# First batch's keys in groups of four through root, scaling and transposes; slot evictions on ScalarE alone; GpSimd's slot fill in pieces

## Chip, cores and metric

The kernel runs on one core of one Trainium2 chip. The metric is the device time of the program in microseconds, the median of the runs; lower is better. Engines are named as the profile names them: PE (TensorE), DVE (VectorE), ACT (ScalarE), POOL (GpSimd), SP (SyncE, which issues the DMAs here).

## What is computed

Two layers of gated cross attention and feed-forward on `x` (4 batches, 256 tokens, 256 wide), with a context of 1601 tokens of width 128 per batch. The change lies wholly in the first layer's attention:

```
y_main, y_dca = y[:, :-16], y[:, -16:]                 # 1585 and 16 context tokens
kv_dca = (y_dca @ Wkv_dca + bkv_dca).reshape(b, 16, 2, H, HD)   # H = 16 heads of HD = 16
k_dca, v_dca = _ln(kv_dca[:, :, 0], kn_dca_w, kn_dca_b), kv_dca[:, :, 1]
q = _ln((x @ Wq + bq).reshape(b, s1, H, HD), qn_w, qn_b)
...        # k, v of y_main likewise, with kn_w, kn_b
_attn(q, k, v) = softmax(q k^T * HD**-0.5) v           # over both sets of keys, apart, then added
```

`_ln` normalises each head's 16 numbers of each token. The mean is taken out in the weights beforehand, so per key and head there remain a sum of squares, a root, a reciprocal and a product. The rest (a mixture of 16 experts, a second attention with 16 heads of 128, a feed-forward with ternary weights) is the same before and after.

## The kernel before

A planner (`Plan`) writes one list of pieces in program order. Every engine walks the list and emits its own part of each piece with semaphore waits, so each engine runs a fixed order. `Plan.stage0` makes the order of the first layer's attention. Its generator `prep(b, banks)` prepares a batch; the loop around it takes one or two steps of `prep` for each step of the scores, and as many steps of `maxima` as the pace wants. For batch 0 the loop runs 19 steps of lead in which there are no scores yet: the kernel's first 100 us. Five of the eight PSUM banks (0, 1, 2, 3, 7) carry the pieces of this preparation, 4 and 5 the maxima.

The pieces of batch 0's preparation, in the order before:

- `kv` (14 of them): a key and value tile of 128 context tokens (tile 12 has 65, tile 13 is the 65-row tail again with the other weights). PE makes `[128, 512]` in a bank; DVE adds the bias to the key half on its way to `kc` (L1315, which reads `wk` from SBUF), then ACT copies the value half to `va` (L1633) and frees the bank.
- `sq`, `ss`: ACT squares four tiles (L1646), DVE sums sixteens into `ss` (L1332). There are five groups: tiles 0 to 3, 4 to 7, 8 to 11, 12 and 13, and the two query tiles.
- `ln1`, `ln2`, `ln3`, `q`: statistics of the tokens (DVE L868, L870), their root (ACT L890), the normalising (DVE L876, L883), the turn on PE (L906) and its copy (ACT L894), and the queries' matmuls with their eviction (DVE L1325).
- `sqrt`: one square root over all of `ss` (ACT L1652), when all five sums are there.
- `scale` (5): DVE takes the reciprocal of a group (L1339) and multiplies the tiles by it (L1342). The queries come first.
- `qt`, `kt`: PE transposes four tiles' half (L999, L1008), ACT writes the result twice, in fp32 and in bf16 (L1660, L1663; L1673, L1674). `qsplit`, `ksplit`: the difference of the two, by DVE (L1364) or GpSimd (L1875) in turn.
- `qr`, `kr`: PE multiplies the split keys by a selection matrix `rsb` and so puts them into the slots of `kst`: eight indices p, each with three tiles of 512 columns and one of 65 (49 main, 16 dca keys). Evictions: `kr` tiles 0, 1, 2 on ACT (L1698), but tile 3 of every p and tile 1 of every odd p on DVE (L1371, L1372; L1375). `qr` by ACT (L1691).
- `bvt`, `bvo`: a bias row through `wo`; then the scores begin.

Later batches get their slots by DMA (`kd`) from SP; their bank `kst1` needs marks in it, which GpSimd writes at the start. Ahead of the list each engine has a few single instructions. On DVE these are the centring of the weights (L1278, L1280), a memset of bank 6 (L1283), and this:

```
for i in range(2):
    V.tensor_scalar(vd[0:TAIL, i, :, 16:17], va[i][0:TAIL, 0, :, 16:17], prm[0:TAIL, 8:9], None,
                    ALU.mult).then_inc(vd_ones, 1)
```

On GpSimd they are memsets and the fill of `kst1` (L1834), one instruction of 8 x 1585 elements per partition and one of 8 x 16, then an add for the bias row (L1837). On ACT they are the tanh of the gates (L1617) and the cast of `rsb` (L1619), both waiting for loads.

## Time and profile before

| | |
|---|---|
| median of three runs | 1677.91 us |
| all three | 1680.65, 1677.91, 1677.08 us |
| the profiled execution's own time | 1681.94 us |
| its span | 1680.6 us |
| its mean granted TensorE clock | 0.945 |
| busy: PE, DVE, ACT, GpSimd | 1460.4, 1244.0, 1101.0, 794.4 us |

The span runs from the first to the last instruction. Busy time of an engine contains time in which a started instruction stands still, so a high share is no proof of work. The granted clock is 1.00 at 2.4 GHz and 0.50 at 1.2 GHz; values between are means over a stretch. A line number is that of the kernel before; several engines share L599, the helper of all matmuls.

### The profile page before, as it was taken

To read this page: it belongs to the slowest core of one execution; us is meant where nothing else is said; L and a number is where in the kernel's file an instruction comes from. 1 tells how busy PE (TensorE), PEld (TensorE's weight loads), DVE (VectorE), ACT (ScalarE), POOL (GpSimd) and SP (SyncE) were. 2 spreads that over 40 slices of the span, in tenths; PEclk is the share of its full clock that TensorE was granted. 3 is DMA by queue.
4 is the path that set the end of the run, shared out by engine and by line. 5 is a ranking of instruction groups with operands and counts; after the bars stand their busy time and mean duration, and the time that the engine had idled before them with its cause. 6 is when DMAs were issued, how large, how long until landed. Compare 5 with 4: busy or idle time off the path is not lost.

```text
span 1680.6 us, 25444 instructions
## 1 busy us (share of the span) xinstructions
PE 1460.4 (87%) x8460; PEld 711.5 (42%) x8460; DVE 1244.0 (74%) x2229; ACT 1101.0 (66%) x1996; POOL 794.4 (47%) x618
## 2 busy tenths in 40 slices
PE   5688887888878797788898989899899999999979
PEld 3243343343333343344444444344544455455445
DVE  6767667667786256478887768899589997788937
ACT  3556656756754755477786668678477775788724
POOL 3014013013130001077766749787486876577823
PEclk8798998998989999799999999999999999999989
DMA  4001200300340100100001000000000000000000
GB/s 154 1 1 29 52 2 2 60 1 2 60 176 1 51 1 5 40 20 6 1 1 32 29 21 6 26 1 1 5 26 1 26 1 1 1 1 1 1 0 26
DMA packets 20489, 36.70 MB, mean 22 GB/s; under 512 B 4898, under 2 KB 15238, under 8 KB 19334
## 3 DMA queue, kind: packets, MB, share of 16 engines
q1 hardware_dynamic: 20358, 35.07, 7.2%
q8 instruction: 68, 1.11, 0.3%
q14 instruction: 63, 0.52, 0.1%
HBM read 26.53 MB, written 1.15 MB: 16 GB/s over the span
## 4 chain that ended last, share of the span: by engine, by line
PE 35%; POOL 9%; issue 7%; DVE 5%; ACT 3%; POOLq 0%; DMA 0%; ACTq 0%; DVEq 0%; SPq 0%
PE BK L599 35%; POOL arena L1929 6%; DVE arena L1559 2%; DVE arena L1542 1%; ACT arena L1806 1%; ACT arena L1814 1%; POOL arena L1926 1%; POOL arena L1904 1%; ACT arena L1799 1%; POOL arena L1935 1%; POOL arena L1914 1%; DVE arena L926 0%; PE BK L906 0%; ACT L1799 0%; DVE arena L1573 0%
## 5 line engine op out<-in xcount | busy, mean ns | idle before, releaser
L599 PE MATMUL BK<-arena 128*128 128x512 bf16 (+14 forms) x8130 | 1414.1, 375 | 188.8 <-DVE arena L1380 43.4
L599 PEld LDWEIGHTS BK<-arena 128*128 128x128 bf16 (+7 forms) x8130 | 674.2, 115 | 897.7 <-issue 218.5
L1929 POOL TENSOR_TENSOR arena<-arena 128x512 f32<-128x512 f32 (+1 forms) x352 | 509.1, 1446 | 178.7 <-ACT arena L1799 154.6
L1559 DVE TENSOR_TENSOR arena<-arena 128x512 bf16<-128x512 f32 (+1 forms) x416 | 513.9, 1244 | 39.8 <-ACT arena L1806 39.1
L1799 ACT ACTIVATE arena<-BK,arena 128x512 f32<-128x512 f32 (+1 forms) x416 | 285.9, 687 | 131.7 <-PE BK L599 116.1
L1707 ACT ACTIVATE arena<-BK 128x512 f32<-128x512 f32 (+1 forms) x416 | 227.2, 604 | 95.0 <-PE BK L599 89.6
L1380 DVE TENSOR_REDUCE arena<-BK 128x1 f32<-128x512 f32 x384 | 244.2, 682 | 53.1 <-PE BK L599 52.2
L1806 ACT CAST arena<-arena 128x512 bf16<-128x512 f32 (+1 forms) x416 | 253.3, 609 | 0.0
L1814 ACT ACTIVATE arena<-BK 128x512 bf16<-128x512 f32 (+1 forms) x256 | 130.0, 508 | 87.7 <-PE BK L599 87.6
L1542 DVE CUSTOM_DVE_ANT_0 arena<-BK,arena 128x512 bf16<-128x512 f32 (+1 forms) x256 | 145.5, 568 | 47.4 <-PE BK L599 41.8
L1848 POOL TENSOR_TENSOR arena<-arena 128x256 f32<-128x256 f32 (+6 forms) x45 | 30.2, 671 | 184.1 <-ACT arena L1646 181.7
L1875 POOL TENSOR_TENSOR arena<-arena 128x512 bf16<-128x512 f32 x24 | 28.2, 1176 | 114.6 <-ACT arena L1674 101.7
L1926 POOL TENSOR_TENSOR arena<-arena 128x512 f32<-128x512 f32 x32 | 45.3, 1417 | 63.5 <-ACT arena L1799 63.5
L1894 POOL TENSOR_TENSOR arena<-arena 128x512 f32<-128x512 f32 x2 | 2.5, 1268 | 117.0 <-DVE arena L1500 117.0
L1507 DVE TENSOR_TENSOR arena<-BK,arena 128x512 f32<-128x512 f32 x32 | 22.0, 687 | 45.9 <-ACT arena L1759 45.7
L1633 ACT COPY arena<-BK 128x256 f32<-128x256 f32 (+1 forms) x52 | 18.9, 372 | 56.1 <-DVE arena L1315 56.1
L1935 POOL TENSOR_TENSOR arena<-arena 128x512 f32<-128x512 f32 x32 | 43.7, 1365 | 9.4 <-DVE arena L1564 9.2
L1315 DVE TENSOR_TENSOR arena<-BK,arena 128x256 f32<-128x256 f32 (+1 forms) x56 | 23.0, 420 | 32.3 <-PE BK L599 32.2
L1579 DVE SCALAR_TENSOR_TENSOR arena<-BK,arena 128x256 f32<-128x256 f32 x8 | 3.9, 484 | 53.6 <-PE BK L599 53.6
L1859 POOL TENSOR_TENSOR arena<-arena 128x1024 f32<-128x1024 f32 (+2 forms) x15 | 23.4, 1591 | 29.6 <-DVE arena L848 29.6
L1788 ACT CAST arena<-BK 128x512 bf16<-128x512 f32 x32 | 18.7, 585 | 25.0 <-PE BK L599 25.0
L1914 POOL TENSOR_TENSOR arena<-arena 128x384 bf16<-128x384 f32 (+1 forms) x20 | 19.7, 1005 | 31.2 <-ACT arena L1781 31.2
(175 smaller groups left out, 850.1 us busy)
## 6 DMA issues: line engine op xcount, KB each, us to landing
arena<-arena SPq DMA_DIRECT2D x144, 50.0 KB, 2.2
arena<-in_ctxT SPq DMA_DIRECT2D x8, 800.5 KB, 4.4
arena<-in_ctxk SPq DMA_DIRECT2D x4, 768.0 KB
arena<-in_wo SPq DMA_DIRECT2D x1, 2048.0 KB, 7.5
arena<-in_wqT SPq DMA_DIRECT2D x1, 2048.0 KB, 7.8
arena<-in_x SPq DMA_DIRECT2D x4, 256.0 KB, 9.4
arena<-in_rsel SPq DMA_DIRECT2D x1, 1024.0 KB, 9.1
arena<-in_rw1T SPq DMA_DIRECT2D x1, 1024.0 KB, 5.0
```

Source lines behind the costliest of these rows:

```text
L599: return T.matmul(out_, lhsT, rhs, start=start, stop=stop, skip_group_check=True)
L1380: V.tensor_reduce(mxp[:, g % 2, u, c:c + 1], BK[i][:, :], AX.X, ALU.max).then_inc(free[i], 1)
L1542: V.tensor_tensor_reduce(out=junk[:, 0:w], in0=BK[i][:, 0:w], in1=rl[:, k % 3, 0:w], scale=1.0, scalar=-3e38, op0=ALU.add, op1=ALU.max, ac ...
L1559: V.tensor_tensor(Pl[k][0:m, :], P1[k][0:m, :], Ph[k][0:m, :], ALU.subtract).then_inc(p_low, 1)
L1707: A.activation(P0[(2 * s + r) % NP][0:m, :], BK[i][0:m, :], ACT.Exp, scale=0.25).then_inc(free[i], 1)
L1799: A.activation(P1[k][0:m, :], BK[i][0:m, :], ACT.Exp, scale=SCALE1, bias=mcb[0:m, b, kt:kt + 1]).then_inc(free[i], 1)
L1806: A.copy(Ph[k][0:m, :], P1[k][0:m, :]).then_inc(p_high, 1)
L1814: A.activation(rl[:, k % 3, 0:w], BK[i][:, 0:w], ACT.Relu).then_inc(free[i], 1)
L1914: t = G.tensor_tensor(ckl[0:m, b, w_, :], ckf[0:m, w_, :], ckh[0:m, b, w_, :], ALU.subtract)
L1926: G.tensor_tensor(acc[:, g % 2, :], P1[(s - 1) % NR][:, :], P1[k][:, :], ALU.add).then_inc(summed1, 1)
L1929: G.tensor_tensor(acc[0:m, g % 2, :], acc[0:m, g % 2, :], P1[k][0:m, :], ALU.add).then_inc(summed1, 1)
L1935: G.tensor_tensor(dg[:, :, :], idn[:, :].unsqueeze(1).to_broadcast([128, 4, 128]), dn[:, 4:8].unsqueeze(2).to_broadcast([128, 4, 128]), AL ...
```

## The change

1. `first_batch` replaces the batch-0 half of `prep`. Each group of four tiles goes on by itself: square, sum, root (`sqrt` now has a group index), reciprocal and scaling, transposes of the first half, splits, while later key tiles are still being made. The queries' group comes last. The statistics of batches 1 to 3 are put between those steps, their roots (`lr`) between the slot evictions of the second half. The second half's transposes follow the first half's slots, as before.
2. The split counters are renumbered for batch 0 (`q_split`, `k_split`): the query split comes after the first half's.
3. All slot tiles of `kr` are evicted by ACT.
4. DVE's two tensor_scalars on `vd` are gone; GpSimd writes the same values with one copy, ahead of the fill. The fill of `kst1` becomes one instruction of 8 x 16 and eight of 1585, after the bias add.
5. On ACT the tanh moves behind `bvt`, the cast of `rsb` to just before the first square.

```diff
+        def first_batch(bank, qs):
...
+            def slots(hf):
+                for p in range(4 * hf, 4 * hf + 4):
+                    if p % 2 == 0:
+                        piece("qr", 0, p, bank=bank())
+                        yield
+                    for c in range(4):
+                        piece("kr", 0, p, c, bank=bank())
+                        if c == 3:
+                            known.add((0, p))
+                        yield
+                    if hf and p < 7:
+                        piece("lr", 0, p - 3)
+
+            for kt in range(6):
+                keys(kt)
+                if kt == 3:
+                    piece("sq", 0, 0)
+                yield
+            piece("ss", 0, 0)
+            next(qs)
...
+            piece("sq", 0, 1)
+            piece("sqrt", 0, 0)
+            keys(8)
+            next(qs)
+            yield
+            keys(9)
+            piece("ss", 0, 1)
+            yield
+            piece("scale", 0, 1)
+            next(qs)
+            keys(10)
+            yield
+            keys(11)
+            piece("sqrt", 0, 1)
+            piece("sq", 0, 2)
+            next(qs)
+            yield
+            turned(0, 0)
+            keys(12)
+            piece("scale", 0, 2)
...
+            piece("ksplit", 0, 0, 3)
+            piece("scale", 0, 0)
+            piece("ln1", 0, 2)
+            yield
+            piece("qt", 0, bank=bank())
+            yield
+            piece("qsplit", 0)
+            piece("ln1", 0, 3)
+            yield
+            yield from slots(0)
+            for c in range(4):
+                turned(1, c)
+                yield
+                piece("ksplit", 0, 1, c)
+            yield
+            yield from slots(1)
...
-            dve.wait_ge(va_ones, 6)
-            dve.wait_ge(ld_prm, 16)
-            for i in range(2):
-                V.tensor_scalar(vd[0:TAIL, i, :, 16:17], va[i][0:TAIL, 0, :, 16:17], prm[0:TAIL, 8:9], None,
-                                ALU.mult).then_inc(vd_ones, 1)
...
-                elif kind == "kr":
-                    b, p, c = arg
-                    if c == 3 or (c == 1 and p % 2):
-                        dve.wait_ge(full[i], n + 1)
...
-            act.wait_ge(ld_g, 16)
-            A.activation(tg[:, :], gat[:, :], ACT.Tanh).then_inc(tanh_done, 1)
-            act.wait_ge(ld_rs, 16)
-            A.copy(rsb[:, :, :, :].rearrange("p a b n -> p (a b) n"), rsf).then_inc(rsb_done, 1)
...
-                    A.activation(ss[:, :, :], ss[:, :, :], ACT.Sqrt, scale=1.0 / 16, bias=cst[:, 1:2]).then_inc(ss_root, 1)
+                    act.wait_ge(*summed(j))
+                    A.activation(ss[0:m, lo:hi, :], ss[0:m, lo:hi, :], ACT.Sqrt, scale=1.0 / 16,
+                                 bias=cst[0:m, 1:2]).then_inc(ss_root, 1)
...
+                    o = kst[b % 2][:, p, :]
+                    act.wait_ge(full[i], n + 1)
+                    if c == 3:
+                        A.activation(o[:, 1536:NMAIN], BK[i][:, 0:TMAIN], ACT.Identity, bias=prm[:, 10:11])
+                        A.activation(o[:, NMAIN:S2], BK[i][:, TMAIN:TAIL], ACT.Identity, bias=prm[:, 11:12]).then_inc(free[i], 1)
+                    else:
+                        A.activation(o[:, 512 * c:512 * c + 512], BK[i][:, :], ACT.Identity, bias=prm[:, 10:11]).then_inc(free[i], 1)
...
-            for lo, hi, col in ((0, NMAIN, 10), (NMAIN, S2, 11)):
-                G.tensor_copy(kst1[:, :, lo:hi], prm[:, col:col + 1].unsqueeze(2).to_broadcast([128, 8, hi - lo])
-                              ).then_inc(k_marked, 1)
+            G.tensor_copy(vd[0:TAIL, :, :, 16:17].rearrange("p i h o -> p (i h) o"),
+                          prm[0:TAIL, 8:9].unsqueeze(2).to_broadcast([TAIL, 32, 1])).then_inc(vd_ones, 2)
...
+            for p in range(8):
+                G.tensor_copy(kst1[:, p:p + 1, 0:NMAIN], prm[:, 10:11].unsqueeze(2).to_broadcast([128, 1, NMAIN])
+                              ).then_inc(k_marked, 1)
```

How the instructions move, at three places. First DVE, from the memset of bank 6 on. Before:

```order
L1283 MEMSET BK 128x512
L1287 TENSOR_SCALAR arena<-arena 65x16 x2
L1315 TENSOR_TENSOR arena<-BK,arena 128x256 x4
L1332 TENSOR_REDUCE arena<-arena 128x64
L1315 TENSOR_TENSOR arena<-BK,arena 128x256 x2
```

In the changed kernel (its key eviction is L1397, its sum L1414):

```order
L1370 MEMSET BK 128x512
L1397 TENSOR_TENSOR arena<-BK,arena 128x256 x6
L1414 TENSOR_REDUCE arena<-arena 128x64
L955 BN_STATS arena<-arena 128x6
L957 BN_AGGR arena<-arena 128x2
```

The two tensor_scalars are gone, six key evictions instead of four come ahead of the first sum, and the token statistics follow it. Second, DVE again, where groups are scaled. Before, from the last statistics on (L1339 is the reciprocal, L1342 the product):

```order
L868 BN_STATS arena<-arena 128x6
L870 BN_AGGR arena<-arena 128x2
L1339 RECIPROCAL arena<-arena 128x32
L1342 TENSOR_TENSOR arena<-arena 128x512
L1339 RECIPROCAL arena<-arena 128x64
L1342 TENSOR_TENSOR arena<-arena 128x1024
L1339 RECIPROCAL arena<-arena 128x64
```

In the changed kernel (L1421 reciprocal, L1424 product, L1407 a query tile's eviction, L1401 that of the dca values):

```order
L1414 TENSOR_REDUCE arena<-arena 128x64
L1421 RECIPROCAL arena<-arena 128x64
L1424 TENSOR_TENSOR arena<-arena 128x1024
L1397 TENSOR_TENSOR arena<-BK,arena 128x256 x2
L1407 TENSOR_TENSOR arena<-BK,arena 128x256
L1397 TENSOR_TENSOR arena<-BK,arena 65x256
L1421 RECIPROCAL arena<-arena 128x64
L1424 TENSOR_TENSOR arena<-arena 128x1024
L1407 TENSOR_TENSOR arena<-BK,arena 128x256
L1397 TENSOR_TENSOR arena<-BK,arena 65x256
L1401 TENSOR_SCALAR arena<-BK,arena 65x16x16
L1414 TENSOR_REDUCE arena<-arena 128x64
```

The product of the first full group now stands after tile 9 and ahead of the eviction of tiles 10 and 11, that of the second between tiles 12 and 13. Third, ACT at the start of the slots. Before (L1691 is a query slot, L1698 a key slot tile; the remaining key tiles are DVE's):

```order
L1682 ACTIVATE arena<-BK,arena 128x16
L1684 ACTIVATE arena<-BK,arena 128x16
L1691 CAST arena<-BK 128x512
L1698 ACTIVATE arena<-BK,arena 128x512 x5
L1691 CAST arena<-BK 128x512
L1698 ACTIVATE arena<-BK,arena 128x512 x5
L1673 ACTIVATE arena<-BK,arena 128x512
L1674 ACTIVATE arena<-BK,arena 128x512
```

In the changed kernel (L1763 query slot, L1772, L1769, L1770 key slots, L1732 and L1735 the transposed queries):

```order
L1754 ACTIVATE arena<-BK,arena 128x16
L1756 ACTIVATE arena<-BK,arena 128x16
L1732 ACTIVATE arena<-BK,arena 128x512
L1735 ACTIVATE arena<-BK,arena 128x512
L1763 CAST arena<-BK 128x512
L1772 ACTIVATE arena<-BK,arena 128x512 x3
L1769 ACTIVATE arena<-BK,arena 128x49
L1770 ACTIVATE arena<-BK,arena 128x16
L1772 ACTIVATE arena<-BK,arena 128x512 x3
L1769 ACTIVATE arena<-BK,arena 128x49
L1770 ACTIVATE arena<-BK,arena 128x16
```

The transposed queries come right ahead of the slots, and each index p has three wide evictions and two narrow ones on ACT. On PE the order from the first `qr` to the first score is the same in both kernels.

## Rows read from the trace of the kernel before

**Rows 1.** Windows: us, busy time (instructions) of each engine, granted clock, DMA share, GB/s.
```profile
20.30:59.70 39.40, 20.18 (x70) 14.38 (x71) 25.54 (x56) 19.10 (x38) 3.58 (x4) 0.67 0.07 21
...
59.70:95.00 35.30, 30.01 (x132) 10.80 (x132) 26.80 (x61) 20.53 (x34) 1.15 (x1) 0.85 0.01 1
...
100.50:560.00 459.50, 387.83 (x3434) 166.18 (x3433) 316.61 (x676) 289.87 (x555) 100.18 (x116) 0.92 0.14 35
```

**Rows 2.** DVE's timeline, 9 to 22 us: start, us, what, count.
```profile
9.99 10.39 DVE L1287 TENSOR_SCALAR arena<-arena 65x16 f32<-65x16 f32 x2
...
20.29 1.40 DVE L1315 TENSOR_TENSOR arena<-BK,arena 128x256 f32<-128x256 f32 x4
```

**Rows 3.** GpSimd's timeline, before the loop and at 110 us.
```profile
8.92 11.43 POOL L1834 CAST arena<-arena 128x12680 bf16<-128x12680 f32 x2 [6.29 <-DMA arena<-in_prm]
...
51.78 1.66 POOL L1875 TENSOR_TENSOR arena<-arena 128x512 bf16<-128x512 f32 x1 [30.67 <-ACT arena L1674]
...
109.52 2.54 POOL L1848 TENSOR_TENSOR arena<-arena 128x512 f32<-128x512 f32 x3 [32.35 <-ACT arena L1646]
```

**Rows 4.** PE's timeline (in brackets: idle before, and what ended it).
```profile
7.12 7.32 PE L599 MATMUL BK<-arena 128*128 128x256 f32 x20 [7.12 <-DMA arena<-in_ctxT]
...
21.22 7.74 PE L599 MATMUL BK<-arena 128*128 128x256 f32 x24 [6.78 <-ACT arena L1633]
...
32.46 0.87 PE L906 MATMUL BK<-arena 128*128 128x128 f32 x4 [3.51 <-ACT arena L1633]
...
54.70 1.01 PE L599 MATMUL BK<-arena 128*128 128x256 bf16 x4
...
59.72 6.34 PE L599 MATMUL BK<-arena 128*128 128x512 bf16 x25 [4.01 <-DVE arena L1364]
```

**Rows 5.** Windows of 1 us, PE alone: us, busy, granted clock, DMA share, GB/s.
```profile
19.00:20.00 1.00, 0.00 (x0) 0.53 0.00 0
...
25.00:26.00 1.00, 1.00 (x4) 0.56 0.00 0
...
33.00:34.00 1.00, 1.00 (x5) 0.50 0.00 0
```

**Rows 6.** DVE by shape, 0 to 100.5 us: count, busy us, mean ns, idle before.
```profile
L1342 DVE TENSOR_TENSOR arena<-arena 128x1024 f32<-128x1024 f32 x3 | 3.7, 1224 | 0.1
...
L1332 DVE TENSOR_REDUCE arena<-arena 128x64 f32<-128x1024 f32 x3 | 3.7, 1220 | 5.2 <-ACT arena L1646 5.2
...
L1339 DVE RECIPROCAL arena<-arena 128x64 f32<-128x64 f32 x3 | 1.6, 544 | 0.0
...
L1342 DVE TENSOR_TENSOR arena<-arena 65x512 f32<-65x512 f32 x1 | 1.3, 1267 | 0.0
...
L1342 DVE TENSOR_TENSOR arena<-arena 128x512 f32<-128x512 f32 x1 | 0.7, 692 | 0.0
```

**Rows 7.** ACT by shape, 0 to 100.5 us.
```profile
L1698 ACT ACTIVATE arena<-BK,arena 128x512 bf16<-128x512 f32 x20 | 13.6, 688 | 12.0 <-PE BK L599 11.9
...
L1673 ACT ACTIVATE arena<-BK,arena 128x512 f32<-128x512 f32 x6 | 4.7, 778 | 5.0 <-DVE arena L1364 3.0 <-PE BK L1008 2.0
...
L1646 ACT ACTIVATE arena<-arena 128x1024 f32<-128x1024 f32 x3 | 3.2, 1062 | 0.0
...
L890 ACT ACT_TABLE_LOAD x1 | 1.3, 1283 | 0.7 <-DVE arena L870 0.7
...
L1679 ACT ACTIVATE arena<-BK,arena 128x49 bf16<-128x49 f32 x2 | 0.8, 400 | 0.0
```

**Rows 8.** DVE by shape, 0 to 100.5 us: its slot evictions.
```profile
L1375 DVE TENSOR_SCALAR arena<-BK,arena 128x512 bf16<-128x512 f32 x4 | 3.0, 749 | 0.9 <-PE BK L599 0.9
...
L1371 DVE TENSOR_SCALAR arena<-BK,arena 128x49 bf16<-128x49 f32 x8 | 2.1, 260 | 3.0 <-PE BK L599 3.0
...
L1372 DVE TENSOR_SCALAR arena<-BK,arena 128x16 bf16<-128x16 f32 x8 | 1.8, 224 | 0.0
```

**Rows 9.** DVE's timeline at 111 us.
```profile
111.65 0.42 DVE L1315 TENSOR_TENSOR arena<-BK,arena 128x256 f32<-128x256 f32 x1 [0.44 <-PE BK L599]
```

More of the change, by code:

```diff
@@ L99, in prep @@
             qs = queries()
+            if b == 0:
+                yield from first_batch(bank, qs)
+                return
             for kt in range(NKT + 1):
@@ L115, in prep @@
             piece("ss", b, 4)
-            if b:
+            yield
+            yield
+            for part in range(4):
+                piece("nw", b, part)
                 yield
-                yield
-                for part in range(4):
-                    piece("nw", b, part)
-                    yield
-            else:
-                for later in range(1, B):
-                    piece("ln1", 0, later)
-                yield
-                piece("sqrt", b)
             for r in range(5):
@@ L1666, in scalar_main @@
                     b, hf_, c = arg
[L1667 removed]
+                    u = k_split(b, hf_, c)
                     act.wait_ge(full[i], n + 1)
```

135 lines of the change are left out of this document (78 added, 57 removed).

## Prediction, made before the changed kernel was run

> **What bounds the kernel now.** I read the windows of the first 100 us first, then each engine's timeline there, then the instructions by shape, and last the waits. The kernel is one in-order program per engine, and the only stretch the change reorders is the first batch's key preparation, before the long loop. First look at DVE [rows 2]: two tensor_scalars of 65x16 elements that write a column of ones into `vd` and take 10.39 us together. Ops of 16 elements elsewhere take about 0.2 us [rows 8]. They start at 9.99 and end at 20.38; the first GpSimd fill of `kst1` runs from 8.92 to 20.35 [rows 3]. So DVE stands still until GpSimd lets go of something, and the key tiles' evictions are queued behind it. PE computes the five key tiles that its banks hold, stops at 14.44 and resumes at 21.22 [rows 4]. In that idle time its granted clock falls from 2.4 to 1.2 GHz, and it is back at about 25.9 us [rows 5].
>
> From 20.3 to 59.7 us nothing is saturated: DVE 25.5 of 39.4 us, ACT 19.1, PE 20.2 [rows 1]. It is a relay: all squares, all sums, one square root, then reciprocal and scaling of each group, transposes, splits. PE gets the first slot matmul at 59.72 [rows 4]. From there to the bias transpose at 95.0 PE is busy 30.0 of 35.3 us, DVE 26.8, ACT 20.5 [rows 1]: PE and DVE (the maxima) alternate as the limit. After 100 us neither the instructions nor their order change, and no load waits for an absolute time, so I take an earlier start as an earlier end, one to one.
>
> **The stall (gain).** The two ops leave DVE; the ones are written by GpSimd, as one small copy ahead of the fill. DVE is free after its memset, about 10.1 us, instead of 20.4. Its next work is the key evictions, 1.40 us for four [rows 2]. They read one operand from PSUM and one from SBUF. Does a GpSimd instruction hold them too? [rows 9] say no: the eviction at 111.65 takes 0.42 us while GpSimd's adds run from 109.52 to 112.06. An op with both inputs in SBUF is another matter: the scaling of 65x512 took 1267 ns against 692 for the larger 128x512 one [rows 6], and it ran at 52.7 beside a GpSimd subtract of 1.66 us [rows 3]. The Trainium skill (SBUF — State Buffer, "Who interferes with whom") has the same division: a Vector instruction contends if it is in a two-port mode, or has two SBUF inputs while GpSimd reads SBUF, and the loser blocks fully. By that rule the new order has one exposed place, the two normalising tensor_scalars about 21 us, if the fill is still running; by it the sum would be one piece of the fill, 1.4 us, less gain.
>
> The fill in nine pieces costs the same, 11.2 us over eight large pieces, 1.4 us each, ending about 21.5. Nobody needs it before the second batch's slot DMAs; what the pieces bound is any hold, to 1.4 us instead of 11.4. I put no hold into the sum and keep 1.4 us for the range.
>
> **The walk to the first slot matmul.** Per-piece times: a key tile on PE. Five took 7.32 us. The next six took 7.74 us, 4.7 of them at 1.2 GHz and 3.1 at 2.4 [rows 4, 5]; with a the price at full clock, 4.7/2a + 3.1/a = 6, so 0.9 us at full clock and 1.8 at half. Square of four tiles 1.06, pair of copies of a transposed slab 1.5, table load 1.28 [rows 7]; sum 1.22, reciprocal 0.54, scaling 1.22 [rows 6]; square root of a group 0.3 to 0.4, as ACT's 49-wide ops [rows 7].
> 1. Key tiles 0 to 3 are evicted as PE gives them; ACT then has the 1.9 us cast of `rsb` (moved behind the copies; it was idle time before) and the first square: to 17.1. PE goes on at full clock through tile 9, about 19.
> 2. Norm statistics, table load, root: 21.1. Apply, PE turn: 23. First group: sum to 18.3, second square 22.8, root 23.1, reciprocal and scaling on DVE to 25.7. PE has idled again from 19 to 22, and in the trace a gap of 3.5 us before 32.5 was followed by a fall to half clock [rows 4, 5], so I price tiles 10 to 13 and the queries low: last tile full at 32.6 (at full clock 29.5).
> 3. Groups three, four and the queries now each run round ACT (square), DVE (sum), ACT (root), DVE (reciprocal, scaling), PE (transpose), ACT (two copies), DVE (split), in a fixed order: third group scaled 32.2, fourth 37.0, tail 41.4, queries 44.5.
> 4. Query transposes 1.1, ACT 1.5, the split on GpSimd 1.2 to 1.7 [rows 3], slot queries 1.0 [rows 4], less a little that overlaps: first slot matmul at 49.5. With tiles at full clock and no wait at the hand-offs, 45.
>
> A check from the other side: DVE's own work in that order, from the memset to the queries' scaling, adds up to about 22 us. At the density that DVE had in the old relay (25.5 in 39.4, 65%) that is 34 us, ending at 44, and 4.7 us of step 4 give 48.8. If DVE never waited, it would be 37. I take 47.5, between the two values of the walk; before it is 59.72. **Gain 12.2 us**, with 10 and 15 as ends, and 22 as the far bound.
>
> Two edits cost nothing: tanh moves behind the bias transpose, where the table for exp was loaded already, and ACT is not the late engine there; the number of ACT's table loads is unchanged. The roots of batches 1 to 3 leave the path (their statistics too: half of them now stand behind the queries' scaling) and are put between slot evictions, three small ACT ops.
>
> **The slot phase.** All 32 slot tiles of the batch are evicted by ACT now; PE's order does not change. DVE loses 3.0 + 2.1 + 1.8 = 6.9 us [rows 8], down to 19.9. ACT takes four more 512-wide at 0.69, eight 49-wide and eight 16-wide at about 0.4 [rows 7], and the three roots: 2.8 + 6.4 + 0.9, so 20.5 becomes 30.6 in a stretch that lasted 35.3 us. PE has 30.0. So the limit passes from PE and DVE to PE and ACT. Were both to overlap perfectly, 4.5 us would be gained; if ACT waits as DVE did, there is a loss of some 2 us. One index costs ACT 3 x 0.69 + 2 x 0.4 = 2.9 us, so the first half, where it has little beside, becomes ACT's (11.6 us for four indices) and should neither win nor lose; the second, which is full of maxima on DVE, should win. I take **2 us gained**.
>
> **Sum.** 12.2 + 2 = 14.2. The profiled execution took 1681.94 us (span 1680.6), so its counterpart is 1667.7; it stands 4 us above the median of the three runs, 1677.91, from which the same sum gives **1663.7**. About 0.2%, 3.4 us, is what a measurement of this kernel tells from no change.
>
> **Rivals.**
> - *Only the stall goes* (0.17). The group-wise relay pays for its hand-offs, four crossings between ACT and DVE per group, and ACT evicting alone eats the rest: start at 50, slot phase 1.5 us longer. For it: in the old relay, too, the engines were idle a third of the time. Gain 8: 1670.
> - *DVE-bound start* (0.10). PE keeps its 2.4 GHz through the keys because it no longer idles 6.8 us; first slot matmul at 44, slot phase 4 us shorter: gain 20, 1658.
> - *Evictions are held after all* (0.04, the slower side). If the key evictions too had to wait for the fill (they read `wk` from SBUF), each would pass between two pieces, 1.4 us apart; eight get through by 21.5. The start then wins some 3 us only, and the slot phase decides: once ACT's 30.6 us plus its waits (ACT's waits for PE there are 12.0 us now [rows 7]) pass 38.3 us, the whole is slower. At their full sum of 42, it is 4 us slower: 1682. Against it stand [rows 9].
> - *The gain is taken back later* (0.05): the long loop from 100 us has PE at 388 of 460 us and a granted clock of 0.92 [rows 1]; if the shifted start changes how often PE falls to 1.2 GHz there, 12 us are 3% of that stretch. The three runs lie within 3.6 us, which speaks against it. Result within 0.2% of 1677.9.
>
> **Numbers.** Forecast case 0.64, gain 11 to 17. Range: the forecast and the first two rivals, with the far bounds left out: 1658 to 1670.5. Faster by over 0.2%: 0.64 + 0.17 + 0.10 = 0.91; within 0.2%: 0.05; slower: 0.04.
>
> **What would show it.** DVE's first key eviction starts at 10 to 10.5 us and takes 0.4; no DVE op before 100 us lasts over 1.6 us; GpSimd shows eight casts of 1.4 us. PE's first idle stretch is near 19 us, not 14.4. First slot matmul 45 to 50 (56 or later: the relay did not shorten). Bias transpose at 78 to 83. From there on the distance between the two traces stays constant to within 2 us; if it does not, the one-to-one carry is wrong. ACT busy in the slot phase about 30 us, DVE about 20; PE's waits there name ACT's slot evictions if ACT is the limit.

## The result, and the profile of the changed kernel

| | before | changed |
|---|---|---|
| median | 1679.28 us (4 runs, 1677.08 to 1680.98) | 1664.46 us (4 runs, 1664.19 to 1665.00) |
| span of the profiled execution | 1680.6 us | 1663.3 us |
| its mean granted clock | 0.945 | 0.945 |

The ratio is 0.9919 with an interval of 0.9899 to 0.9938. The medians are 14.8 us apart; the ratio, which is estimated over all runs and isn't the quotient of the medians, is worth 13.6 us, its interval 10 to 17. The forecast was 14.2.

The same events in both traces, in us:

| event | before | changed | moved by |
|---|---|---|---|
| first key eviction on DVE | 20.29 | 10.16 | 10.1 |
| first slot eviction on ACT | 60.77 | 50.84 | 9.9 |
| bias transpose on PE | 94.96 | 83.78 | 11.2 |
| first exp on ACT (scores start) | 100.46 | 89.28 | 11.2 |
| end of the span | 1680.6 | 1663.3 | 17.3 |

So the head gave 11.2 us, three less than forecast, and the rest of this pair of traces 6.1 us, where nothing was forecast. DVE's timeline, which answers [rows 2] (columns as there):

```profile
9.76 0.48 DVE L1370 MEMSET BK<- 128x512 f32 x1
10.16 0.41 DVE L1397 TENSOR_TENSOR arena<-BK,arena 128x256 f32<-128x256 f32 x1
...
21.47 1.34 DVE L970 TENSOR_SCALAR arena<-arena 128x256 f32<-128x256 f32 x2
...
24.77 1.23 DVE L1424 TENSOR_TENSOR arena<-arena 128x1024 f32<-128x1024 f32 x1
```

The key eviction starts as the memset ends and takes 0.41 us, though GpSimd, which answers [rows 3], is busy beside it:

```profile
8.91 0.84 POOL L1908 COPY arena<-arena 65x32 f32<-65x32 f32 x1 [6.28 <-DMA arena<-in_prm]
9.77 0.72 POOL L1911 TENSOR_TENSOR arena<-arena 128x256 f32<-128x256 f32 x1
...
10.67 11.67 POOL L1915 CAST arena<-arena 128x1585 bf16<-128x1585 f32 x8
```

PE, for [rows 4]:

```profile
7.33 11.36 PE L680 MATMUL BK<-arena 128*128 128x256 f32 x40 [7.33 <-DMA arena<-in_ctxT]
23.65 1.09 PE L993 MATMUL BK<-arena 128*128 128x128 f32 x4 [4.97 <-ACT arena L1700]
24.53 4.93 PE L680 MATMUL BK<-arena 128*128 128x256 f32 x12
...
29.74 2.75 PE L680 MATMUL BK<-arena 128*65 128x256 f32 x12
...
45.03 1.09 PE L1086 MATMUL BK<-arena 128*128 128x128 f32 x4 [2.57 <-DVE arena L1424]
48.94 9.19 PE L680 MATMUL BK<-arena 128*128 128x256 bf16 x40 [2.82 <-issue]
```

Ten tiles now run without a stop, to 18.69; before, five did. The last row begins with the query slots (128x256) and goes over into the key slots, whose first matmul starts at 49.74 (59.72 before). The 2.82 us ahead of it end 0.1 us after GpSimd's query split, which takes 1.15 us from 47.68. ACT's timeline:

```profile
10.64 1.28 ACT L1700 ACT_TABLE_LOAD   x1 [10.64 <-DVE arena L1397]
...
19.65 1.28 ACT L977 ACT_TABLE_LOAD   x1 [1.87 <-DVE arena L957]
...
50.84 0.69 ACT L1772 ACTIVATE arena<-BK,arena 128x512 bf16<-128x512 f32 x1 [0.27 <-PE BK L680]
```

The first row is new at this place. In the kernel before, the first table load stood at the tanh, at 0.73, long before the tanh itself:

```profile
0.73 1.28 ACT L1617 ACT_TABLE_LOAD   x1 [0.73 <-PEq L2295]
10.94 0.20 ACT L1617 ACTIVATE arena<-arena 128x4 f32<-128x4 f32 x1 [8.92 <-DMA arena<-in_gates]
```

Windows (columns as in [rows 1]). Of the changed kernel, the relay from about 20 us (where the old one began) to the first key slot's matmul, DVE's stretch from its memset to the queries' scaling, the slot phase from its first ACT eviction to the bias transpose, and the sixteen score groups from the first `mneg` of DVE to the last; then the last two of the kernel before:

```profile
20.00:49.74 29.74, 12.89 (x50) 9.56 (x51) 20.21 (x43) 15.11 (x31) 5.04 (x4) 0.65 0.09 28
9.76:44.89 35.13, 19.93 (x79) 15.49 (x77) 23.81 (x49) 20.09 (x38) 14.12 (x11) 0.77 0.30 109
50.84:83.78 32.94, 28.07 (x130) 10.13 (x128) 22.35 (x41) 25.93 (x56) 1.16 (x1) 0.87 0.00 0
78.74:531.61 452.87, 388.11 (x3351) 168.06 (x3352) 323.98 (x691) 286.95 (x550) 100.41 (x116) 0.91 0.14 36
```

```profile
60.77:94.96 34.19, 28.92 (x129) 10.34 (x127) 26.76 (x61) 20.40 (x33) 1.15 (x1) 0.86 0.01 1
89.58:548.80 459.22, 386.98 (x3351) 166.35 (x3352) 326.25 (x695) 284.34 (x543) 100.18 (x116) 0.92 0.14 35
```

DVE is busy for 68% of the first window, and for 68% of the second; in the old relay it was 65% [rows 1]. The relay itself didn't get shorter: from the first key eviction to the first key slot's matmul it takes 39.6 us (10.16 to 49.74), and it took 39.4 (20.29 to 59.72). It starts 10.1 us sooner and keeps its length; what it would be without the new order is seen below. The slot phase is 1.25 us shorter. What ACT and PE do in it, by shape (count, busy us, mean ns, idle before); ACT from 0 to 89.3 us, PE from 50.8 to 83.8:

```profile
L1772 ACT ACTIVATE arena<-BK,arena 128x512 bf16<-128x512 f32 x24 | 16.0, 697 | 4.9 <-PE BK L680 4.6
...
L1769 ACT ACTIVATE arena<-BK,arena 128x49 bf16<-128x49 f32 x8 | 2.4, 305 | 2.3 <-PE BK L680 2.3
...
L1770 ACT ACTIVATE arena<-BK,arena 128x16 bf16<-128x16 f32 x8 | 2.3, 282 | 0.0
```

```profile
L680 PE MATMUL BK<-arena 128*128 128x512 bf16 x47 | 15.7, 461 | 1.5 <-DVE arena L1446 1.5
L680 PE MATMUL BK<-arena 64*128 64x512 bf16 x32 | 10.5, 421 | 3.4 <-DVE arena L1451 3.1
```

PE's waits there name DVE's maxima (L1451) and its splits (L1446), never ACT's slot evictions. PE was and stays the nearly full engine, with DVE's maxima behind it.

Two questions follow. Which part of the change moves the first exp by how much? And where do the three to six us after 89 us come from: does an earlier start gain more than itself?

### The profile page after: what moved, and what is told of

It is laid out like the page before. It is cut to its first block, busy times and chain, and to the rows that moved or that the text cites. A ratio compares the mean times of both kernels' runs of the same rounds, so it can differ in the third digit from the quotient of the medians.

```text
span 1663.3 us, 25453 instructions
## 1 busy us (share of the span) xinstructions
PE 1459.2 (88%) x8460; PEld 712.2 (43%) x8460; DVE 1226.7 (74%) x2207; ACT 1108.0 (67%) x2020; POOL 795.7 (48%) x626
## 3 DMA queue, kind: packets, MB, share of 16 engines
HBM read 26.53 MB, written 1.15 MB: 17 GB/s over the span
## 4 chain that ended last, share of the span: by engine, by line
PE 35%; POOL 9%; issue 7%; DVE 5%; ACT 3%; POOLq 0%; DMA 0%; ACTq 0%; DVEq 0%; SPq 0%
PE BK L680 35%; POOL arena L2008 6%; DVE arena L1630 3%; DVE arena L1613 1%; ACT arena L1881 1%; ACT arena L1889 1%; POOL arena L2005 1%; POOL arena L1983 1%; ACT arena L1874 1%; POOL arena L2014 1%; POOL arena L1993 1%; DVE arena L1013 0%; PE BK L993 0%; DVE arena L1644 0%; ACT L1874 0%
## 5 line engine op out<-in xcount | busy, mean ns | idle before, releaser
L1451 DVE TENSOR_REDUCE arena<-BK 128x1 f32<-128x512 f32 x384 | 244.3, 684 | 57.0 <-PE BK L680 56.0
L2005 POOL TENSOR_TENSOR arena<-arena 128x512 f32<-128x512 f32 x32 | 44.9, 1403 | 62.3 <-ACT arena L1874 62.3
L1397 DVE TENSOR_TENSOR arena<-BK,arena 128x256 f32<-128x256 f32 (+1 forms) x56 | 23.5, 422 | 36.9 <-PE BK L680 36.9
L1993 POOL TENSOR_TENSOR arena<-arena 128x384 bf16<-128x384 f32 (+1 forms) x20 | 19.7, 1006 | 32.6 <-ACT arena L1856 32.6
```

The source lines that it names most:

```text
L1451: V.tensor_reduce(mxp[:, g % 2, u, c:c + 1], BK[i][:, :], AX.X, ALU.max).then_inc(free[i], 1)
L1993: t = G.tensor_tensor(ckl[0:m, b, w_, :], ckf[0:m, w_, :], ckh[0:m, b, w_, :], ALU.subtract)
L2005: G.tensor_tensor(acc[:, g % 2, :], P1[(s - 1) % NR][:, :], P1[k][:, :], ALU.add).then_inc(summed1, 1)
```

## Experiments: the parts of the change

"Start" below is the time of the first exp in each kernel's trace (100.46 before, 89.28 changed), a marker that needs no long run.

**The ones by GpSimd alone**, added to the kernel before; the fill stays one instruction.

```diff
-            for i in range(2):
-                V.tensor_scalar(vd[0:TAIL, i, :, 16:17], va[i][0:TAIL, 0, :, 16:17], prm[0:TAIL, 8:9], None,
-                                ALU.mult).then_inc(vd_ones, 1)
...
+            G.tensor_copy(vd[0:TAIL, :, :, 16:17].rearrange("p i h o -> p (i h) o"),
+                          prm[0:TAIL, 8:9].unsqueeze(2).to_broadcast([TAIL, 32, 1])).then_inc(vd_ones, 2)
```

> The kernel before, with one edit: GpSimd writes the ones into vd with one copy ahead of its single fill, DVE's two tensor_scalars are gone. Theory (DVE's stall is the hold of those two ops by the GpSimd fill, and nothing else is held): first key eviction at 10 to 10.5 us, PE's first idle gap after tile 8 or 9 and not at 14.4, first slot matmul at about 51, time 8.5 us below before (7 to 10). Rival (key evictions, which read wk from SBUF, are held by the fill too): evictions still start at 20.4, no gain. Rival (the stall was cover for other work): gain under 5 us.

Median 1668.25 us (7 runs), ratio 0.9946 (0.9926 to 0.9965), so 9 us by the ratio (6 to 12), where 8.5 were expected. DVE's timeline, then GpSimd's:

```profile
9.97 0.41 DVE L1310 TENSOR_TENSOR arena<-BK,arena 128x256 f32<-128x256 f32 x1
```

```profile
9.48 10.99 POOL L1831 CAST arena<-arena 128x12680 bf16<-128x12680 f32 x2
```

An eviction that reads PSUM and SBUF runs through beside one GpSimd instruction of 10.8 us; it isn't held. The stall of 10.4 us is gone, but the start moves by 4.1 us only, to 96.39; the first key slot's matmul comes at 54.79, not at the 51 expected. So the time came out as expected and the way to it did not. PE's timeline shows where the other six go:

```profile
15.85 5.76 PE L599 MATMUL BK<-arena 128*128 128x256 f32 x24 [1.51 <-ACT arena L1628]
26.99 1.08 PE L906 MATMUL BK<-arena 128*128 128x128 f32 x4 [5.38 <-ACT arena L1628]
27.86 6.71 PE L599 MATMUL BK<-arena 128*128 128x256 f32 x20
42.48 1.09 PE L999 MATMUL BK<-arena 128*128 128x128 f32 x4 [7.91 <-DVE arena L1337]
```

Against [rows 4]: the eleventh tile ends at 21.61 instead of 28.96 (7.4 us gained, the rest was PE's own pace); the token turn starts at 26.99 instead of 32.46 (5.5; PE now waits 5.38 us for ACT, where it waited 3.51); the last key work ends at 34.57 instead of 39.09 (4.5; these matmuls take 6.71 us instead of 5.97). Each station of the relay ate a piece: from the first key eviction to the first key slot it now takes 44.8 us (9.97 to 54.79), instead of 39.4.

**The fill in pieces alone**, the ones left on DVE.

```diff
-            for lo, hi, col in ((0, NMAIN, 10), (NMAIN, S2, 11)):
-                G.tensor_copy(kst1[:, :, lo:hi], prm[:, col:col + 1].unsqueeze(2).to_broadcast([128, 8, hi - lo])
-                              ).then_inc(k_marked, 1)
+            G.tensor_copy(kst1[:, :, NMAIN:S2], prm[:, 11:12].unsqueeze(2).to_broadcast([128, 8, NDCA])
+                          ).then_inc(k_marked, 1)
+            for p in range(8):
+                G.tensor_copy(kst1[:, p:p + 1, 0:NMAIN], prm[:, 10:11].unsqueeze(2).to_broadcast([128, 1, NMAIN])
+                              ).then_inc(k_marked, 1)
```

> The kernel before, with one edit: the GpSimd fill in one small and eight large pieces, DVE's two tensor_scalars stay. Theory (the hold lasts as long as one GpSimd instruction): the two ops wait for a piece each at most, together 0.6 to 2.9 us instead of 10.39; gain 7 to 9 us. Rival (GpSimd keeps the port through back-to-back instructions): 10.4 us stay, no gain.

Median 1672.74 us (10 runs), ratio 0.996 (0.994 to 0.998), 6.7 us by the ratio, just under the 7 to 9 expected; start 96.48. DVE's timeline, then GpSimd's:

```profile
9.94 1.15 DVE L1287 TENSOR_SCALAR arena<-arena 65x16 f32<-65x16 f32 x2
10.98 0.79 DVE L1315 TENSOR_TENSOR arena<-BK,arena 128x256 f32<-128x256 f32 x2
```

```profile
9.54 11.67 POOL L1836 CAST arena<-arena 128x1585 bf16<-128x1585 f32 x8
```

The two ops take 1.15 us in all, against 10.39 [rows 2], beside a fill that is as long as ever. They end at 11.09, as the first piece ends (11.04). So the stall lasted as long as the GpSimd instruction that it met, and eight instructions of 1.5 us let DVE in. Either edit alone removes the whole stall; the change has both.

**The new order alone**: the changed kernel with the two tensor_scalars back on DVE, one fill (not in the lines below), and the slot evictions shared as before. The moved tanh and cast stay in it.

```diff
+            for i in range(2):
+                V.tensor_scalar(vd[0:TAIL, i, :, 16:17], va[i][0:TAIL, 0, :, 16:17], prm[0:TAIL, 8:9], None,
+                                ALU.mult).then_inc(vd_ones, 1)
...
+                    if c == 3 or (c == 1 and p % 2):
+                        dve.wait_ge(full[i], n + 1)
```

> The changed kernel's order (groups of four, roots one by one, queries last), but the stall is put back (ones by two DVE tensor_scalars, one fill) and the slot evictions are shared with DVE as before. Theory (the parts add up: the stall is most of the gain at the start, grouping the rest): first slot matmul 55 to 57, gain 3 to 4 us over before. Rival (the grouping is the gain and the stall is partly cover): gain over 7. Rival (grouping only pays once the stall is gone): within 1 us of before.

Median 1674.50 us (10 runs), ratio 0.9962 (0.9944 to 0.998); start 98.50. The stall is back, `10.12 10.39` for the two ops, and the new order is worth 2.0 us at the start. The first key slot's matmul comes at 57.21 (55 to 57 expected). In the time it is 4.1 us by the medians and 6.4 by the ratio (3 to 9), which doesn't tell the 3 to 4 expected from more.

**All but the evictions**: the changed kernel with slot tiles shared between DVE and ACT again.

```diff
+                elif kind == "kr":
+                    b, p, c = arg
+                    if c == 3 or (c == 1 and p % 2):
+                        dve.wait_ge(full[i], n + 1)
...
-                    act.wait_ge(full[i], n + 1)
-                    if c == 3:
...
+                    if c != 3 and not (c == 1 and p % 2):
+                        act.wait_ge(full[i], n + 1)
```

> The changed kernel with slot evictions shared between ACT and DVE as before (tile 3 of every index and tile 1 of every odd one on DVE). Theory (giving all to ACT took work from the limit, DVE, in the second half): 1 to 2 us slower than the changed kernel, the distance from first slot matmul to the bias transpose back at about 35 us. Rival (ACT alone is now the limit there): faster than the changed kernel by up to 2 us.

Median 1664.95 us (4 runs), ratio 0.9905 (0.9875 to 0.9935); start 90.30. Its slot phase in the windows:

```profile
50.18:84.80 34.62, 29.41 (x129) 10.59 (x128) 26.94 (x61) 20.93 (x36) 1.15 (x1) 0.83 0.00 1
```

The phase takes 34.62 us against 32.94 (about 35 was expected), so the evictions on ACT shorten it by 1.7 us; 1.0 us of that is left at the first exp, since this build reached its first slot 0.7 us sooner. In the total (1664.95 against 1664.46) the 1 to 2 us expected can't be seen.

Put together, the start moves by:

| in the kernel | start | gained |
|---|---|---|
| stall gone (ones, or pieces) | 96.39, 96.48 | 4.1, 4.0 |
| new order, stall kept | 98.50 | 2.0 |
| both | 90.30 | 10.2 |
| both, evictions on ACT | 89.28 | 11.2 |

4.1 and 2.0 alone, 10.2 together: 4 us belong to neither part. In the relay's length (first key eviction to first key slot's matmul) it is 39.4 us before, 44.8 with the stall gone and the old order, 39.2 with the stall gone and the new one (9.90 to 49.08). So the new order is what keeps the relay from growing when its front starts sooner. My reading, which no run isolates: with the old order the early keys wait for the one root over all groups; with the stall the groups arrive too late for the order to matter much.

## Experiments: what an earlier start is worth

The changed kernel once more, and with DVE kept busy by 11, 22 or 36 chained memsets of 128x256 ahead of the reciprocal of the queries' group. Nothing else is touched, so only the start moves.

```diff
+                        for _ in range(36 if r == 0 else 0):
+                            V.memset(yo[:, :], 0.0).then_inc(dve_chain.sem, dve_chain.up())
+                            dve.wait_ge(dve_chain.sem, dve_chain.n)
                         V.reciprocal(
```

> The changed kernel, measured again beside the three that follow, to see its own spread: 1664.5, within 2 us. It is the zero of the delay series.

> The changed kernel with eleven chained DVE memsets of the unused tile yo ahead of the queries' reciprocal (about 0.33 us each, 3.6 us in all, the profile will tell): everything from the query scaling on starts later. Theory (one-to-one carry on average): the first exp moves by the delay, and the median time by the delay, 1668. Rival (the loop's length depends on when it starts): the time moves by another amount, between 0 and 7 us.

> As r1_delay_3 with 22 memsets, about 7.2 us. Theory: first exp and time later by the same 7.2, 1671.7. Rival: time off that line by over 2 us.

> As r1_delay_3 with 36 memsets, about 11.8 us, so that the first exp falls where it did before, at 100 to 101 us. Theory (one-to-one): 1676, that is 3 us below the kernel before, so that before had 3 us in its loop which do not come from its start. Rival (the loop's length depends on the start alone): 1679, as before.

| kernel | start | median (runs) | ratio to the kernel before |
|---|---|---|---|
| changed again | 89.22 | 1665.13 (6) | 0.9924 (0.9904 to 0.9944) |
| 11 memsets | 94.08 | 1672.98 (12) | 0.9973 (0.9955 to 0.9991) |
| 22 memsets | 98.85 | 1677.82 (12) | 0.9993 (0.9974 to 1.0011) |
| 36 memsets | 102.81 | 1679.90 (12) | 1.0007 (0.9988 to 1.0025) |

A memset costs 0.39 us, not the 0.33 that the expectations took, so each delay came out longer than planned. DVE's row in the last one:

```profile
43.67 13.98 DVE L1421 MEMSET arena<- 128x256 f32 x36
```

The start moves by 4.9, 9.6 and 13.6 us and the time by 7.8, 12.7 and 14.8. At about the same start as the kernel before (98.85 and 102.81 around 100.46) the new order takes the same time (1677.8 and 1679.9 around 1678.7, the 29 runs of it in this set). So, to within the 3 us of these intervals, the new order has no worth of its own behind the start: what the change gains, it gains by starting the scores earlier. One to one from the repeat, the starts make 1670.0, 1674.8 and 1678.7 us; measured are 1673.0, 1677.8 and 1679.9. So step by step it looks less even: the first 5 us cost 8, the last 4 cost 2. With 3 us of interval on each ratio neither step is clearly off one to one.

The traces of this series carry the delay evenly through the scores. The stretch from DVE's first `mneg` to its last, in the kernels with 11, 22 and 36 memsets (the repeat of the changed kernel, 456.05 us, follows below):

```profile
83.54:539.59 456.05, 386.06 (x3351) 166.21 (x3352) 325.02 (x690) 286.41 (x550) 100.16 (x116) 0.92 0.14 36
```

```profile
88.31:543.81 455.50, 383.94 (x3351) 165.44 (x3352) 324.47 (x690) 286.42 (x550) 100.21 (x116) 0.93 0.14 36
```

```profile
92.27:548.34 456.07, 388.68 (x3351) 167.29 (x3352) 325.91 (x690) 286.78 (x550) 100.18 (x116) 0.92 0.14 36
```

A start moved by 4.9 to 13.6 us leaves its length the same to within 0.6 us: in these executions the rival that the loop's length depends on its start doesn't show.

Over all fourteen traces of this study (each first exp against the median of its runs), the least-squares line has a slope of 1.15 with a standard error of 0.09, and the medians lie within 4.5 us of it, 1.8 us in the root mean square. The largest miss is the kernel with only the ones on GpSimd, 4.5 us below, with 3.3 us of interval on its own ratio. One to one fits as the mean (1 lies within two standard errors), and a single kernel may be off by a few us either way.

Where that scatter sits: the stretch from the first `mneg` to the last has the same 3351 matmuls in all of them; the counts of DVE and ACT differ only by a few slot evictions at its head. Its window in the second trace of the changed kernel, in that of the ones by GpSimd alone, and in the one-fill kernel that follows:

```profile
78.68:534.73 456.05, 387.08 (x3351) 167.33 (x3352) 325.87 (x690) 286.57 (x550) 100.02 (x116) 0.92 0.14 36
```

```profile
85.51:535.43 449.92, 385.66 (x3351) 166.61 (x3352) 325.74 (x695) 284.46 (x543) 100.28 (x116) 0.92 0.14 36
```

```profile
77.54:526.74 449.20, 383.15 (x3351) 165.74 (x3352) 324.94 (x690) 286.75 (x550) 100.28 (x116) 0.93 0.14 36
```

The changed kernel itself took 452.87 us here in one execution and 456.05 in the other; over the fourteen traces it is 449.2 to 459.2, and the longest is the profiled execution of the kernel before. Against its repeat, the 6 us gained in the loop shrink to 3.2. Inside the stretch the two first traces gain and give back by turns, as the clock goes. Two neighbouring pieces, before and changed (each between the same two `mneg`s):

```profile
157.42:186.89 29.47, 23.98 (x233) 9.71 (x231) 18.89 (x37) 24.79 (x50) 6.15 (x6) 0.94 0.33 61
186.89:211.11 24.22, 19.54 (x201) 6.88 (x201) 17.42 (x34) 14.61 (x28) 0.00 (x0) 0.93 0.16 30
```

```profile
145.97:177.03 31.06, 26.48 (x233) 10.34 (x232) 19.12 (x38) 24.84 (x50) 6.16 (x6) 0.84 0.35 65
177.03:198.04 21.01, 18.39 (x201) 6.75 (x201) 17.34 (x33) 14.62 (x28) 0.00 (x0) 1.00 0.14 26
```

At 0.84 instead of 0.94 the changed kernel loses 1.6 us, at 1.00 instead of 0.93 it gains 3.2. After 548.80 and 531.61 the two traces run in step: from there to the same place near the end, 1634.0 and 1616.7, it is 1085.2 and 1085.1 us.

## Experiments: is there a better version?

Four edits of the changed kernel: the fill as one instruction again; the queries' group scaled ahead of the tail's split and of most of the later batches' statistics (which the lines below leave out), and the first index's key slots ahead of the first query slots; a one-element square root as ACT's very first instruction; the second and third together.

```diff
-            for p in range(8):
-                G.tensor_copy(kst1[:, p:p + 1, 0:NMAIN], prm[:, 10:11].unsqueeze(2).to_broadcast([128, 1, NMAIN])
-                              ).then_inc(k_marked, 1)
+            for lo, hi, col in ((0, NMAIN, 10), (NMAIN, S2, 11)):
+                G.tensor_copy(kst1[:, :, lo:hi], prm[:, col:col + 1].unsqueeze(2).to_broadcast([128, 8, hi - lo])
+                              ).then_inc(k_marked, 1)
```

> The changed kernel with GpSimd's fill in one large and one small piece again (ones ahead of it, bias add behind it). Theory (once the ones are off DVE the pieces do nothing): first exp at 89 to 90.5 us, time as the changed kernel, 1665, within its spread. Rival (two-port and two-input DVE ops are held by it now): DVE's normalising tensor_scalars, at 21 us, wait for the end of the fill, at most 1.5 us; 1666.5.

```diff
             piece("sqrt", 0, 4)
             turned(0, 3)
+            piece("scale", 0, 0)
             yield
             piece("ksplit", 0, 0, 3)
-            piece("scale", 0, 0)
...
-                    if p % 2 == 0:
+                    if p % 2 == 0 and p:
                         piece("qr", 0, p, bank=bank())
...
+                    if p == 0:
+                        piece("qr", 0, p, bank=bank())
```

> The changed kernel with another order at the end of the relay: the queries' reciprocal and scaling go ahead of the tail's split and of the second batch's statistics, and the four slot tiles of index 0 go ahead of the first query slots on PE, to cover the wait for the query split. Theory (the last link of the relay is the queries' chain, with every engine idle beside it): first slot eviction at 46 instead of 50.8, first exp 4.4 us earlier, 85. Rival (ACT, which now evicts everything, is the limit right behind): first exp under 2 us earlier. The time follows by about as much, 1661, if the loop carries it on.

```diff
+            act.wait_ge(cst_set, 2)
+            A.activation(cst[:, 2:3], cst[:, 1:2], ACT.Sqrt)
```

> The changed kernel with one tiny square root on ACT ahead of everything, so that the table for it is loaded while the loads are under way: one table load instead of two before the slots. Theory (the second load, 1.28 us, stands on the path between the token statistics and the normalising): normalising and all behind it 1.3 us earlier, first exp at 88. Rival (PE's key tiles hide it): first exp unchanged.

> s2_queries_earlier and s3_one_table together. Theory (both are on the path, one behind the other): first exp at 83.5, 5.7 us before the changed kernel's; time 1659 to 1660. Rival (they overlap): 85.

| kernel | first slot eviction | start | median (runs) | ratio |
|---|---|---|---|---|
| changed | 50.84 | 89.28 | 1664.46 (4) | 0.9919 (0.9899 to 0.9938) |
| one fill | 49.79 | 88.08 | 1661.81 (4) | 0.9909 (0.9873 to 0.9945) |
| queries earlier | 45.13 | 85.14 | 1661.07 (6) | 0.9894 (0.9865 to 0.9923) |
| one table | 49.66 | 87.72 | 1662.30 (6) | 0.9907 (0.9877 to 0.9938) |
| queries and table | 45.15 | 85.21 | 1660.22 (6) | 0.9891 (0.9860 to 0.9921) |

*One fill.* Once the ones are off DVE the pieces bring nothing; the start is even 1.2 us earlier, and 0.8 us ahead of the 89 to 90.5 expected. Its normalising ops and GpSimd's fill:

```profile
20.76 0.73 DVE L970 TENSOR_SCALAR arena<-arena 128x256 f32<-128x256 f32 x2
```

```profile
10.24 11.08 POOL L1913 CAST arena<-arena 128x12680 bf16<-128x12680 f32 x2
```

The big instruction ends at 21.0 (it starts at 10.24 and lasts 10.75), so the two ops meet its last 0.2 us and the small one behind it, and take 0.73 us. In the changed kernel they start at 21.47, meet the last piece (20.8 to 22.3) and take 1.34. But the 1.2 us aren't shown to come from the fill. The root of the token statistics already stands 0.71 us sooner here (20.23 against 20.94), by as much as PE's first ten tiles end sooner (17.98 against 18.68), and that end scatters from 17.98 to 19.61 us over the ten traces that share this front. From the root to the turn on PE it takes 2.66 us here and 2.71 in the changed kernel: the 0.6 us of hold cost PE 0.05.

*Queries earlier.* PE begins its slots at 43.84 instead of 48.94, without the 2.82 us of wait ahead of them:

```profile
42.68 1.09 PE L1089 MATMUL BK<-arena 128*128 128x128 f32 x4 [0.54 <-DVE arena L1427]
43.84 9.83 PE L683 MATMUL BK<-arena 128*128 128x512 bf16 x40
```

(These are the rows of the kernel with both edits; the other's are the same to 0.1 us.) The slots start 5.1 us sooner (the first key slot's matmul 5.9, since it now also stands ahead of the query slots), the first maxima 4.5 sooner (DVE at 49.98 instead of 54.50), the first exp 4.1, to 85.14, as expected (85). The forty matmuls at its head take 9.8 us instead of 9.19.

*One table.* ACT's timeline:

```profile
0.73 1.28 ACT L1688 ACT_TABLE_LOAD   x1 [0.73 <-PEq L2376]
...
20.32 0.29 ACT L977 ACTIVATE arena<-arena 128x2 f32<-128x2 f32 x1 [1.83 <-DVE arena L957]
```

One load at 0.73, in idle time, serves copies, squares and roots up to the exp; those at 10.64 and 19.65 are gone. The start is 1.6 us earlier by itself (87.72, where 88 was expected), and not at all on top of the queries' edit (85.21 against 85.14; 83.5 had been the theory, 85 the rival). The pair of kernels with the queries' edit, without and with the table edit, tells why. Their root runs at 20.61 and 19.33: 1.28 us sooner, which is the root's own load. The load ahead of the first copies cost nothing there: PE's first ten tiles end at 18.36 with it and at 18.41 without. Their normalising ops:

```profile
21.14 1.62 DVE L973 TENSOR_SCALAR arena<-arena 128x256 f32<-128x256 f32 x2
```

```profile
20.37 2.32 DVE L973 TENSOR_SCALAR arena<-arena 128x256 f32<-128x256 f32 x2
```

Both pairs end just behind the fill's last piece (22.76 and 22.69, the piece at 22.30 and 22.22), and PE turns the tokens at 23.60 and 23.53. The first op of the second pair takes 2.00 us by itself. It starts while one piece runs, which ends at 20.78, and isn't let in then: the next piece holds it to 22.22. So the fill in pieces ate the table's gain, and a hold isn't bounded by one piece, as it was in the kernel with only the fill in pieces. The table edit and the queries' edit with one fill weren't run together. In the kernel with the table edit alone the turn comes 0.27 us sooner, and the three tiles behind it take 4.27 us instead of 4.93, at a mean granted clock of 0.64 instead of 0.55; there lies more than half of its 1.6 us.

The version with both edits has the lowest median of the study and starts the scores 4.1 us before the changed kernel, as the one with the queries' edit alone does. Its 1660.2 us against 1664.5 and 1665.1 is about that, but the intervals of the ratios overlap, so the start is shown and the total is likely, not shown.

## Why the prediction held, step by step

- **The stall and its cause: right.** First eviction at 10.16 (10 to 10.5 said), 0.41 us (0.4 said). No DVE op before 100 us lasts over 1.6 us. Either edit alone removes it, which the prediction didn't say: it gave the pieces no part in the gain. The pieces took 1.5 us each, not 1.4, and ended at 22.3, not 21.5.
- **Evictions not held: right**, shown beside one instruction of 10.8 us. The slower rival falls with it.
- **The exposed place: right, and it cost next to nothing.** The normalising ops take 1.34 us instead of 0.73: 0.6 us held, of at most 1.4 said, and PE's turn comes 0.05 us later (0.2 in the repeat of this kernel). "What the pieces bound is any hold" failed in a later kernel, where one op was held through two pieces (2.00 us). The Trainium skill (SBUF — State Buffer, "Who interferes with whom") has Vector work in a two-port mode, or with two SBUF inputs against a GpSimd instruction that reads SBUF, contend with GpSimd, and the one that issues second block fully. The 0.6 us at 21.47 agrees; the one-fill kernel, whose ops met only the fill's last 0.2 us, shows no hold.
- **The walk, right; the choice from it, wrong by 2.4 us.** Said against measured (ends of the scalings): token root 21.1, 21.2; first group 25.7, 26.0; last tile 32.6, 32.5; the next two key groups ("third" and "fourth" there, though they are the second and third) 32.2, 32.95 and 37.0, 37.45; tail 41.4, 41.9; queries 44.5, 44.9; first key slot's matmul 49.5, 49.74. The step that failed is "I take 47.5, between the two values of the walk": the walk was right to 0.3 us at its end (0.75 at the worst station), and its lower value, 45, with full clock and no wait at the hand-offs, had no part in what happened. The check by DVE's density was right as well: it took 22 us of work at 65%, an end at 44 and 48.8 for the slots; measured are 23.8 us at 68%, an end at 44.89. Had the forecast stayed with either, it would have had 10 to 11 us here. PE's 24.53 4.93 is three tiles at 1.6 us (1.8 priced), at a mean granted clock of 0.55; the query tiles after it ran at full clock, but the groups no longer waited for them. The gain was 10.0 us (59.72 to 49.74), at the lower end of the 10 to 15 given.
- **"Two edits cost nothing": right, as far as the traces show.** The number of table loads is unchanged, as said. The tanh had kept its load in idle time at 0.73; without it a load stands at 10.64, ahead of the first key copies. Without that load PE's first ten tiles end no sooner (18.41 against 18.36). The load that does cost, 1.28 us at the root, the kernel before has too (at 26.12).
- **The slot phase: right in sign, 1.25 us instead of 2.** ACT has 25.9 us, not 30.6, and DVE 22.35, not 20. ACT's 49-wide and 16-wide evictions took 0.305 and 0.282 us, where the term took 0.4 from another op of that width, L1679, which has a scale column besides the bias column; that is 1.7 of the 4.7 us. Most of the rest is that neighbouring ops overlap, and busy time counts the overlap once: in the sixteen narrow evictions 4.7 us of durations add only 3.1 us of busy time. What DVE lost shrinks in the same way: its slot evictions, 6.9 us of durations, had added 5.4 us of busy time. The Trainium skill (ScalarE: Activation LUTs, "What ACT_TABLE_LOAD costs") prices an activation with one such column at 280 ns and 0.833 ns per element, and 93 ns more for a second; that makes, as an estimate from this page, 321 and 293 ns here, near the rows, and would have made the term 1.5 us smaller. And the limit is not ACT: PE waits 3.1 us for maxima (L1451). The shared-eviction kernel puts the term at 1.7.
- **One to one: right as a mean, and it made up for the rest.** "The distance between the two traces stays constant to within 2 us" failed: it went from 10.84 at the first `mneg` to 17.19 at the last and stayed there. The head gave 11.2 us; the medians differ by 14.8 and, with the second set, by 13.6. The slope over the fourteen traces, 1.15, makes 12.9 of 11.2. That the total came within 0.8 us of the forecast is thus partly luck: an overestimate of 3 us at the head against some 2 to 4 us that the medians gained behind it, where the scatter is as large.
- **Rivals.** "Only the stall goes" said 50 for the start of slots, which is what came, and 1670 for the time, which didn't: it had the slot phase 1.5 us longer. Its mechanism fell too: with only the stall gone and the old order the slots start at 54.79, so the grouping earns 5.7 us of those 10. The DVE-bound start fell: first key slot's matmul at 49.74, not 44, and PE didn't keep its clock (0.55 from 24.53 to 29.46).

What stays open is whether the first 5 us of delay really cost 8, and whether the kernel with the ones on GpSimd really lies 4.5 us below the line: neither is clear of the intervals. In the traces the loop's length goes with the clock that its pieces get, as the two windows above show, but no run here sets that by itself.

## What to carry to other kernels

If a tiny op shows a duration tens of times its work, look for what ends at the same moment on GpSimd. To move the op or to cut the GpSimd instruction into pieces both freed it here, and one of the two was enough; of the two, moving the op is the surer, since pieces back to back held another op through two of them. Price a relay station by station and then trust the walk: a stall of 10 us ahead of one is not worth 10 us until the stations behind it can use the earlier work, so a restart of the front and a finer order behind it should be tried together. Read the gain at a marker just behind the change, where a trace tells 1 to 2 us (less only if the marks ahead of it agree); behind a long loop whose length goes with the clock a pair of traces can't tell 5.

## What the runs showed of the hardware

- The time of one and the same program goes with its mean granted clock: of the 62 runs of the kernel before that stood beside the experiments, the fastest took 1671.8 us at 0.949 and the slowest 1685.2 us at 0.937, and the least-squares line over them is about 1 us less for each 0.001 of clock.
- Where ACT's table load runs isn't told by the instruction's place alone. The tanh's ran at 0.73, 8.9 us ahead of the tanh, which waited for a DMA. The loads at 10.64 and 19.65 ran only once DVE had released the copy and the root they belong to, and so stood right ahead of these. No run here tells what makes the difference. An early one-element square root put the load at 0.73, and no copy, square or root needed another.
- GpSimd's fill costs 10.75 us as one instruction of 12680 elements per partition and 1.5 us for each of eight of 1585; 11.1 us in all with the small piece, and 11.7 for the eight with their overlaps. Cutting it up costs 0.6 us or a little more.
- A DVE tensor_scalar that meets a GpSimd instruction can be held past the end of that one and through the next: 2.00 us from 20.37, where pieces of 1.5 us end at 20.78 and 22.22. In the kernel with only the fill in pieces two such ops were let in after the first piece, at 11.04. What decides between the two is open.
